# First loads of an attention block issued while the projections run, one block fewer in front of it, and bounds taken with one root

## The reference, cut to what matters

```python
x = L0_attn_x                                        # 4 sequences of 1024 tokens, 128 wide, float32
x = x + _layernorm(_L0_attn_ref(_layernorm(x), ...)) # attention over channels, one head
x = x + _layernorm(_L0_ffn_ref(_layernorm(x), ...))  # feed-forward with ternary weights
x = x + _layernorm(_L1_attn_ref(_layernorm(x), ...)) # softmax attention: 16 heads of 8, with rotary positions
x = x + _layernorm(_L1_ffn_ref(_layernorm(x), ...))  # 24 experts, top 2, in 4 groups of tokens
# inside _L1_attn_ref, per sequence and head:
q = _apply_rope(proj(Wq, bq), cos, sin) * scale
k = _apply_rope(proj(Wk, bk), cos, sin)
attn = softmax(einsum('bhsd,bhtd->bhst', q, k), axis=-1)
out = einsum('bhst,bhtd->bhsd', attn, v)
```

## Time and profile before

| | |
|---|---|
| median of the runs | 1156.36 us (1156.05 to 1159.06) |
| the profiled execution | 1163.83 us, of which its span is 1161.9 us |
| busy in the span | PE 907.8 us (78%), ACT 781.1 (67%), DVE 597.1 (51%), PEld 428.5 (37%), POOL 360.5 (31%) |
| mean granted clock of PE | 0.89 of full speed |
| DMA | 109.67 MB, mean 94 GB/s |
| the stage of the projections | 191.70 (first load) to 293.81 us (flag written) |
| the stage of the attention | 306.97 (first score product) to 800.06 us (last division) |

### The profile page before, as it was taken

How to read it: one execution, slowest core, us unless ns; L and a number is a source line. 1 busy time by engine, 2 the same in 40 slices (tenths; PEclk the granted TensorE clock), 3 DMA queues, 4 the chain that set the end, 5 groups by cost and what they waited for, 6 DMA issues and landing times. The chain is left out here.

```text
span 1161.9 us, 19219 instructions
## 1 busy us (share of the span) xinstructions
PE 907.8 (78%) x6570; PEld 428.5 (37%) x6570; DVE 597.1 (51%) x2007; ACT 781.1 (67%) x1186; POOL 360.5 (31%) x332
## 2 busy tenths in 40 slices
PE   3754984765399999999989999998869878696650
PEld 3642763332021222222222222232357556365550
DVE  7387856888100444444443325342353236686557
ACT  1233342436499999999989999995565665675530
POOL 6312433445300000000000000222576477766743
PEclk8676986887699999999999999998959999898885
DMA  3000001235751212121111212245777655677741
GB/s 102 1 1 1 1 1 59 68 96 143 238 160 43 61 42 60 41 60 42 44 36 43 61 42 61 54 117 152 238 127 171 204 175 160 179 238 136 157 107 52
DMA packets 91259, 109.67 MB, mean 94 GB/s; under 512 B 11997, under 2 KB 62814, under 8 KB 91050
## 3 DMA queue, kind: packets, MB, share of 16 engines
q1 hardware_dynamic: 77128, 79.56, 23.1%
q0 software_dynamic: 12416, 27.80, 11.5%
q10 hardware_dynamic: 1634, 1.30, 0.4%
HBM read 68.90 MB, written 39.71 MB: 93 GB/s over the span
## 5 line engine op out<-in xcount | busy, mean ns | idle before, releaser
L1513 ACT ACTIVATE s_e<-s_ps 128x1024 f32<-128x1024 f32 x512 | 476.7, 1069 | 17.3 <-PE s_ps L1681 16.6
L1694 PE MATMUL s_acc<-s_e,s_v 128*32 128x512 f32 x2048 | 274.7, 609 | 0.7 <-ACT s_e L1513 0.7
L1135 POOL DMA_INDIRECT x_in<-x_tokens,rows_of x72 | 71.8, 997 | 464.8 <-DVE rows_of L1294 427.5
L1681 PE MATMUL s_ps<-s_q,s_k 51*128 51x512 bf16 x1024 | 180.6, 388 | 32.9 <-DMA s_k<-in_ones_row 13.3
L1681 PEld LDWEIGHTS s_ps<-s_q,s_k 51*128 51x128 bf16 x1024 | 41.2, 93 | 282.9 <-ACT s_e L1513 254.4
L2118 ACT ACTIVATE e_ht<-e_pn,ln_hid 128x288 f32<-128x288 f32 x192 | 85.9, 504 | 34.8 <-PE e_pn L2014 34.7
L2030 PE MATMUL e_py<-w,e_ht 128*96 128x128 f32 x768 | 108.7, 292 | 0.0
L2030 PEld LDWEIGHTS e_py<-w,e_ht 128*96 128x96 f32 x768 | 98.2, 179 | 0.0
L2000 PE MATMUL e_ph<-w,e_xt 128*32 128x512 f32 x576 | 79.0, 621 | 11.4 <-ACT e_hs L2085 6.8
L2014 PE MATMUL e_pn<-ident,e_hs 128*128 128x128 f32 x216 | 42.0, 314 | 44.8 <-ACT e_ht L2118 23.2
L1135 POOL DMA_INDIRECT e_ya<-y_rows,take x64 | 65.2, 1018 | 38.0 <-issue 29.9
(11 more groups left out here) (422 smaller groups left out, 1419.3 us busy)
## 6 DMA issues: line engine op xcount, KB each, us to landing
h_rows<-e_hs SPq DMA_DIRECT2D x54, 256.0 KB, 3.4
s_q<-parts_q SPq DMA_DIRECT2D x64, 96.0 KB
w<-in_w SPq DMA_DIRECT2D x1, 6144.0 KB, 20.7
s_k<-parts_k SPq DMA_DIRECT2D x62, 96.0 KB
h_rows<-x_res SPq DMA_DIRECT2D x18, 256.0 KB, 3.0
y_rows<-e_ys SPq DMA_DIRECT2D x24, 192.0 KB
s_k<-parts_k SPq DMA_DIRECT2D x62, 64.0 KB
parts_q<-b_parts SPq DMA_DIRECT2D x16, 192.0 KB, 2.7
```

Source lines behind the costliest of these rows:

```text
L1135: nc.gpsimd.indirect_dma_start(dst, None, rows, bass.IndirectOffsetOnAxis(ap=idx, axis=0), compute_op=op).then_inc(R["landed"][k % FLIGHT] ...
L1513: nc.scalar.activation(E[g % 4][:, 2 * pair:2 * pair + 2, :], pS[BUFFER["score", 2 * g + pair]][:].rearrange("p (a s) -> p a s", a=2), ACT ...
L1681: last = nc.tensor.matmul(pS[BUFFER["score", 2 * g + pair]][:, a * CH:(a + 1) * CH], K[c % 2][rows, pair, j * P:(j + 1) * P], Q[c % 2][row ...
L1694: last = nc.tensor.matmul(acc[hu % 2][32 * h:32 * h + 32, :], V4[c % 2][:, j, h, :], E[g % 4][:, h, :], start=j == 0, stop=j == TB - 1)
```

## The change

1. The tensors of K and Q of the attention, and the semaphores of their loads, now exist before the projections. In the projections, SP loads the rows that were ones (now -1, four DMAs) after the padding of the shifts, and the queries and keys of unit 0 after row 8 and those of unit 1 after row 10 (`first_unit`). The attention then has only the shifts of these two units to load. ACT issues no DMA there any more.
2. SP no longer waits at the end of the projections for its stores to land. The attention waits for what it reads (`stored`): the parts and shifts of batch 0 ahead of the first shifts, the other batches behind the small loads and ahead of W1, the padding at the start.
3. `exact_maxima` is now a class whose parts stand inside the attention's block: on SP behind the loads of unit 1, on DVE and PE at the head of their lists. The block and its barrier are gone. POOL clears the semaphores inside the attention, behind `token_numbers`.
4. The bounds: DVE takes two maxima per batch from `N2` (keys, then queries), ACT takes the root of the squared query norm times the key maximum in one instruction and writes `sh` itself; the sign is now in the K rows. The test at the end is on squares: one product of 16x4 and one maximum.
5. Buffers of the expert layers (`XT`, `HT`, one of two `YS`) lie in the space of K and Q.

```diff
@@ second_projections, SP
             for b in range(B):
                 for s in range(1, 3):
-                    sp.dma_start(S["sh"][b, s], pad[:]).then_inc(sh_out, 16)
+                    sp.dma_start(S["sh"][b, s], pad[:]).then_inc(pad_out, 16)
+            for i in range(2):
+                for a in range(2):
+                    sp.dma_start(R["K"][i][64 * a + ROW_SHIFT:64 * a + ROWS_QK, :, :],
+                                 A["minus_ones"].rearrange("s (h t) -> s h t", h=2)).then_inc(R["ones_in"], 16)
+
+            def first_unit(c):
+                for i in range(2):
+                    sp.wait_ge(part_out[i], 2 * 16 * (6, 2)[i])
+                load_queries(sp, S, R["Q"][c], 0, c, slice(0, CH), R["qk_in"][c])
+                load_keys(sp, S, R["K"][c], 0, c, R["qk_in"][c])
...
             for i in range(2 * NCH):
                 parts_row(i)
                 if i % 4 == 3 and i >= 7:
                     shift_row(i // 4 - 1)
+                if i in (8, 10):
+                    first_unit(i // 2 - 4)
             shift_row(B - 1)
-            sp.wait_ge(sh_out, B * 3 * 16)
-            for i in range(4):
-                sp.wait_ge(part_out[i], B // 2 * 2 * 16 * (6, 2)[i % 2])
@@ second_projections, ACT
             def shift(b):
-                act.wait_ge(m2_done, b + 1)
-                nc.scalar.activation(m2[:], m2[:], ACT.Sqrt).then_inc(m_done, 1)
+                act.wait_ge(kmax_done, b + 1)
+                nc.scalar.activation(sh[:, b, :], N2[:, 0, b * L:(b + 1) * L], ACT.Sqrt,
+                                     scale=top[:, 1, b:b + 1]).then_inc(sh_done, 1)
@@ second_projections, DVE
-                c.run(nc.vector.tensor_reduce(kmax[:, b:b + 1], N2[:, 1, tb], AX.X, ALU.max))
-                if b >= 1:
-                    v.wait_ge(sh_done, b)
-                nc.vector.tensor_scalar(m2[:], N2[:, 0, tb], kmax[:, b:b + 1], None, ALU.mult).then_inc(m2_done, 1)
-
-            def shifts(b):
-                v.wait_ge(m_done, b + 1)
-                c.mark(nc.vector.tensor_reduce(mmax[:, b:b + 1], m2[:], AX.X, ALU.max))
-                nc.vector.tensor_scalar(sh[:, b, :], m2[:], -1.0, None, ALU.mult).then_inc(sh_done, 1)
+                nc.vector.tensor_reduce(top[:, 1, b:b + 1], N2[:, 1, tb], AX.X, ALU.max).then_inc(kmax_done, 1)
+                c.mark(nc.vector.tensor_reduce(top[:, 0, b:b + 1], N2[:, 0, tb], AX.X, ALU.max))
...
-            c.run(nc.vector.tensor_reduce(ok[:, 0:1], mmax[:], AX.X, ALU.max))
+            c.run(nc.vector.tensor_tensor(top[:, 0, :], top[:, 0, :], top[:, 1, :], ALU.mult))
+            c.run(nc.vector.tensor_reduce(ok[:, 0:1], top[:, 0, :], AX.X, ALU.max))
@@ the exact maxima: the same instructions, now ExactMaxima.sync, .vector, .tensor
+        slow = sp.value_load(R["flag"], min_val=0, max_val=1)
+        with sp.If(slow > 0):
...
@@ second_scores, SP
+            def stored(b):
+                for i in range(2):
+                    sp.wait_ge(R["part_out"][2 * (b % 2) + i], (b // 2 + 1) * 2 * 16 * (6, 2)[i])
+                sp.wait_ge(R["shift_out"][b], 16)
+
             def load(k, c):
...
-                load_queries(sp, S, Q[c % 2], b, c, ts, qk_in[c % 2])
+                if half == 0 and c == 0:
+                    stored(b)
+                if k or c >= 2:
+                    load_queries(sp, S, Q[c % 2], b, c, ts, qk_in[c % 2])
                 load_shifts(sp, S, Q[c % 2], b, c, ts, qk_in[c % 2])
-                if k or c:
+                if k or c >= 2:
                     load_keys(sp, S, K[c % 2], b, c, qk_in[c % 2])
...
                 if n == 1:
+                    exact.sync(sp)
                     sp.dma_start(R["wo"][:], A["wo_t"]).then_inc(w_in, 16)
...
                     sp.dma_start(R["lnh"][:], A["ln_hid"]).then_inc(R["ln_in"], 16)
+                    for b in range(1, B):
+                        stored(b)
                     sp.dma_start(W1[:], A["w1"].rearrange("e d f -> d e f")).then_inc(R["w_in"], 16)
@@ second_scores, ACT
-            load_keys(act, S, K[0], 0, 0, qk_in[0])
-            for i in range(2):
-                for a in range(2):
-                    act.dma_start(K[i][64 * a + ROW_SHIFT:64 * a + ROWS_QK, :, :],
-                                  A["ones_row"].rearrange("s (h t) -> s h t", h=2)).then_inc(ones_in, 16)
```

More of the change, by code:

```diff
@@ L1448, in second_scores @@
         late_bank = lambda i: pS[BUFFER["late", i]][:, 0:CH]
-        qk_in = [sem(f"qk_in{i}") for i in range(2)]
         scores, exp_done, av_done, v_staged, acc_read, tr_mm, o_done, rec_done = (sem("s_" + n) for n in (
@@ L1570, in _ @@
             choice = Choice(nc, v, c, R, W, 0)
+            exact.vector(v)
             v.wait_ge(v_zero, 4)
@@ L1674, in score @@
                 if j == 0 and pair == 0:
-                    if first and c < 2:
-                        pe.wait_ge(ones_in, 16 * 4)
+                    if first and c == 0:
+                        pe.wait_ge(R["ones_in"], 16 * 4)
                     pe.wait_ge(qk_in[c % 2], k * (2 * LOAD) + LOAD * (c // 2 + 1))
@@ L1757, in half @@
                         pe.wait_ge(w_in, 48)
+            exact.tensor(pe)
             over_halves(pe, half)
@@ L1782, in expert_layers @@
         XS = R["XS"]
-        XT = [sb(f"e_xt{i}", [P, TPB * P]) for i in range(2)]
+        kept = Room(R["qk"][:])
+        XT = [kept.take(TPB * P) for i in range(2)]
+        HT = [kept.take(TPB * P) for c in range(FC)]
+        YS = [kept.take(EB, D)[0:ROWS], sb("e_ys1", [ROWS, EB, D])]
         HS = sb("e_hs", [P, NT, FF])
-        HT = [sb(f"e_ht{c}", [P, TPB * P]) for c in range(FC)]
-        YS = [sb(f"e_ys{i}", [ROWS, EB, D]) for i in range(2)]
         YA = sb("e_ya", [P, GT, 2, D])
@@ L2331, in build @@
         S["sh"] = nc.dram_tensor("shifts", (B, 3, HEADS, L), BF16, kind="Internal").ap()
+        R["qk"] = sb("qk", [P, 3 * L])
+        kept = Room(R["qk"][:])
+        R["K"], R["Q"] = ([kept.take(2, n, dtype=BF16) for i in range(2)] for n in (L, CH))
+        for n in ("ones_in", "pad_out"):
+            R[n] = ctx.enter_context(nc.semaphore("b_" + n))
+        for n, count in (("qk_in", 2), ("part_out", 4), ("shift_out", B)):
+            R[n] = [ctx.enter_context(nc.semaphore(f"b_{n}{i}")) for i in range(count)]
         second_projections(nc, R, A, S)
-        exact_maxima(nc, R, S)
         R["w_in"] = ctx.enter_context(nc.semaphore("experts_in"))
```

185 lines of the change are left out of this document (93 added, 92 removed).

## The result

The changed kernel takes 1151.2 us (median of 20 runs, 1146.3 to 1157.85) against 1156.58 for the kernel before beside it (20 runs, 1149.36 to 1162.46): a ratio of 0.9948, 95% interval 0.9935 to 0.9962. That is faster by 5.4 us, where 11.5 were forecast, and 0.7 us above the end of the range. The profiled execution took 1151.21 us, of which its span is 1149.5.

What follows compares the result with a forecast made beforehand. The bound was a chain: SP's stores, landing, barrier, an idle block, barrier, load. First score from 306.97 to 295.5, 11.5 us earlier, unit 2 costing 0, gave 1144.9 from 1156.36 us; range 1142 to 1150.5.

Steps and rivals of the forecast that it cites:

- The chain to the first score: From projections to attention: SP's stores, barrier, shift loads and landing put the first score at 295.5, 11.5 us earlier.
- So SP, not the flag, ends the block: End of the projections: SP's queue ends at 291.9, the flag at about 288.2, so this part gives 3.5 us, not 5.6.
- What comes late next: unit 2: Unit 2's loads on SP, behind W1 and `w2`: W1 1.5 us behind the first score, 3.1 us later relative to the scores.
- reading the flag and the jump 0.7: On SP before the small loads and W1: flag and jump over the exact maxima cost an estimated 0.7 us.
- The bound of 2.3 us for the jump: Jumps over the exact maxima take at most 2.3 us, from about 295.4 to 297.75 in the kernel before.
- I put the cost at 0: Unit 2's later loads in the attention cost 0 us, with 2 us kept for the range.
- the 2.2 us to spare: In the attention before: DMA engines empty from 334, PE finished unit 1 at 336.20, leaving 2.2 us for later loads.
- The signs named in the prediction: Wrong if first score later than 299, ACT gap over 2 us at unit 2, or experts' length changed over 3 us.
- Unit 2 starves ACT: Rival in the attention: the 11.5 gain stands at the first score, 3 us given back at unit 2: 1147.9; chance 0.06.
- The rule on jumps: SP's jump, by instruction prefetch: nearer 2.3 than 0.7 us, W1 1.6 us later still, the spare overdrawn by 2.5.
- The slow rival: Early loads in the projections block SP's queue: first score at 309.5, kernel 1158.9 us; chance 0.04.
- Nothing moves: Rival at the first score: something other than the rows of ones and the loads holds it; 1156 us, chance 0.04.

Runs made afterwards that it cites:

- the run with early units: Changed kernel with the loads of units 0 and 1 behind rows 5 and 7 of the projections instead of 8 and 10: 1148.01 us, 0.9914 of before.
- the first two experiments: Changed kernel with SP's flag read and jump moved behind W1 and `w2`: 1148.26 us; changed kernel without the exact maxima on SP, DVE and PE: 1147.11 us.
- the rows for 2.63 and 4.84 us of the table: W1's issue behind the first score: 2.63 with SP's conditional part cut to one wait (1144.25 us), 4.84 in the changed kernel's second profile (1205.43 us).

## Why the prediction was wrong

*The chain to the first score: right, with some luck in the sizes.* The last `kmax` was put at 284.5 and starts at 284.75; the flag at 288.2 (288.21); SP's end at 291.9 (292.59), the row of stores starting 1.05 us later than I took (271.65 for 270.6); the opening at 292.4 (292.99); the first score at 295.5 (295.63). SP's last store to SP's first load took 0.52 us, the barrier and my 0.3 together having been put at 0.8. "So SP, not the flag, ends the block" is borne out by the run with early units. The early loads took what was worked out: 1.02 + 2.22 us for the second eight, for 3.1. The jumps on PE and DVE cost nothing that can be seen. The luck is in the absolute times: in the six other profiles of the same projections the flag is written 1.6 to 3.0 us earlier and the first score stands between 292.71 and 294.56. What holds in all seven is 0.5 us from SP's last store to its first load and 2.5 to 2.6 us from the opening to the first score.

*The step that failed is in "What comes late next: unit 2": its term "reading the flag and the jump 0.7".* The pause was 3.58 us. I had W1 1.5 us behind the first score; it was 4.86. Of the 3.4 us between, 2.9 are the jump, 0.4 SP's later start of its shifts, 0.25 the small loads, and -0.2 shifts and score. The bound of 2.3 us for the jump was taken from the gap between two blocks, in which POOL's clears end last, and SP's queue was not isolated in it. The measured price is beyond it. With W1 that late the last keys of unit 2 were issued 30.1 us behind the first score, ACT waited 4.29 us, and the forecast "I put the cost at 0" fell with its term.

At my own number the 0 was right. W1 1.47 us behind the first score left no wait at unit 2, and 1.64 us left 0.16. So the 2.2 us to spare and the three buffers did cover the 3.1 us by which I had W1 later relative to the scores; they did not cover 6.4.

*A term that was missing:* the 0.3 to 0.9 us that ACT waits ahead of its 8th exponential in ten of the twelve profiles with the whole change or most of it, while PE still runs at the lower clock for part of the time. I let the attention shift as a whole.

*The signs named in the prediction.* The gap over 2 us at unit 2 came (2.82 us). So did a change of the experts' stage by more than 3 us (6.5), but that sign was drawn too narrow: the stage varies by 7.7 us between profiles of the same code.

*How the loss comes about.* W1 and `w2` need the full DMA engines for some 20 us (W1 landed 20.2 us after its issue), and the queue holds whatever is issued behind them: from W1's issue to the end of the queries of unit 2 it is 22.3 us here, 23.1 in the kernel before, 22.6 and 22.1 in the first two experiments. All later steps follow W1. From the end of the issue of unit 2's last keys to the score 3.8 us pass (325.72 to 329.54).

*The rival "Unit 2 starves ACT" was the right one*, with its 3 us mis-sized: 4.29 at unit 2, 5.26 in the whole first part. I gave it 0.06. The gain of 11.5 less 5.26 makes 6.2 us, against 5.88 in the trace and 5.4 in the medians.

*The rule on jumps.* The pause at a jump over more than 200 instructions is 3.58 us and at one over a single instruction 1.22. The rule of the Trainium skill (Runtime: NRT & Kernel Launch, "Instruction fetch mechanics"), that a taken jump out of the fetched window waits for a fetch by DMA, agrees with that difference of 2.4 us. That SP waited for such a fetch is argued, not shown: the DMA view lists two or three packets of the kind `instruction` in the long pauses and two in the short one, and doesn't say for which engine. The jump at its upper bound of 2.3 us would have put W1 3.1 us behind the first score; between the rows for 2.63 and 4.84 us of the table that is 1.5 to 4.3 us of waits in place of none.

*The slow rival* (SP's queue blocked by the early loads) did not occur. *"Nothing moves"* neither.

*What the parts are worth.* Bounds alone 0.37% (0.06 to 0.69); the wait for landing 1.6 us of opening; the early loads: without them the kernel is no faster than before (1.0024, 0.9989 to 1.006). The block that is gone and its barrier were not tried alone. These don't add up to 5.4 since the parts share SP's queue and the stall at unit 2.

## What to carry to other kernels

When a chain is shortened, follow the same queue one step past the point that was gained: a big load that was issued ahead of the first use may now be behind it, and everything queued after it inherits the delay. A conditional part that is never taken isn't free on a queue engine: put it behind the loads that others wait for, not ahead. A load of many pieces that nobody needs soon belongs behind the small loads that are needed next; that one move was worth at least as much as the change itself by the medians (0.9869 with it and 0.9948 without, where the kernel before takes 1157 us; 0.9906 and 0.9962 on another chip), of which the traces assign 4.8 and 4.7 us to the first part.

## What was not expected of the hardware

- A jump that is taken on SP over a long part takes 3.50 to 3.64 us in the seven profiles in which it stands ahead of the small loads. Behind `w2`, with the DMA engines at a share of 1.05, SP is back only 6.6 us after the issue of `w2` (306.66 to 313.27). The wait for PE's scores, which comes behind the jump, can't have held it: without a jump it released SP at 310.36, in a kernel whose first score is 0.9 us later. So the jump seems to have taken longer while W1 and `w2` filled the DMA engines; one profile shows it.
- `w2` held SP's queue for 9.4 to 11.7 us directly behind W1 and for 0.85 us with the DMA engines at a share of about 0.5 (the run with `w2` behind unit 3): what a DMA costs its issuer depends on what is in flight.
- PE's granted clock fell to 0.66 for the 5 us behind a stall of 4 us in the middle of the attention and was back at 1.00 in the next 5.
- The same program takes 1157 us on one chip and 1205 to 1209 on two others, and in the profiles of the kernels here nearly all of the difference lies in the experts' stage (350 to 360 against 401 to 411 us).
